# A selective-scan kernel on one core: the copy of each state's last column moves from ScalarE to GpSimd

## The reference, cut to what matters

```
def step(h, inp):
    u_t, d_t, b_t, c_t = inp
    dA = jnp.exp(d_t[..., None] * A)
    h = dA * h + (d_t * u_t)[..., None] * b_t[:, :, None, :]
    y = jnp.einsum('bkdn,bkn->bkd', h, c_t)
    return (h, y)
```

## Time and profile before

| | |
|---|---|
| time, median of 3 runs | 12323.96 us (12319.58 to 12334.21) |
| the profiled execution, its own time | 12312.74 us |
| its span from first to last instruction | 12310.8 us |
| DVE busy, share of the span | 88% |
| PE busy, share of the span | 86% |
| POOL busy, share of the span | 77% |
| ACT busy, share of the span | 72% |

### The profile page before, as it was taken

One profiled execution on the slowest core, in us unless ns is written; L12 is line 12 of the kernel. 1 busy time (PEld: TensorE's weight loads), 2 busy tenths in 40 slices (PEclk: granted clock), 3 DMA queues, 4 the chain that ended last, 5 costly groups with the idle time before them and its releaser, 6 DMA issues. The chain is left out here.

```text
span 12310.8 us, 117469 instructions
## 1 busy us (share of the span) xinstructions
PE 10629.6 (86%) x33046; PEld 4749.1 (39%) x33046; DVE 10864.5 (88%) x7695; ACT 8817.2 (72%) x18292; POOL 9515.3 (77%) x4213
## 2 busy tenths in 40 slices
PE   7888888888888888888888888888888888888888
PEld 2443334343344433434334443334433344334443
DVE  7999779997799978999789997899968999689996
ACT  5777667776677766777667776677766777667776
POOL 4999459994599945999459994599936999369993
PEclk9999989999899998999989999999998999999999
DMA  4677446764467644677446774477745677356773
GB/s 140 214 222 214 117 133 215 221 215 110 134 214 222 214 109 139 215 221 214 104 143 215 221 214 101 148 215 219 214 97 149 216 220 215 94 153 215 219 215 91
DMA packets 677497, 2203.72 MB, mean 179 GB/s; under 512 B 165008, under 2 KB 167056, under 8 KB 665424
## 3 DMA queue, kind: packets, MB, share of 16 engines
q1 hardware_dynamic: 676848, 2196.22, 61.3%
HBM read 2098.86 MB, written 67.11 MB: 176 GB/s over the span
## 5 line engine op out<-in xcount | busy, mean ns | idle before, releaser
L1309 POOL TENSOR_TENSOR state<-state,c_sb 128x1024 f32<-128x1024 f32 x3072 | 7180.7, 2363 | 610.5 <-ACT carry L1143 528.5
L1065 PE MATMUL ps<-state,wt 128*128 128x512 f32 x12288 | 5863.5, 614 | 350.5 <-ACT ya L1136 233.4
L1278 DVE TENSOR_TENSOR_SCAN state<-decay,carry,ps 128x1024 f32<-128x1024 f32 x1728 | 4006.7, 2340 | 41.1
L1065 PEld LDWEIGHTS ps<-state,wt 128*128 128x128 f32 x12288 | 2324.5, 196 | 2778.8 <-issue 2105.3
L1199 ACT ACTIVATE decay<-delta,a_neg 128x1024 f32<-128x1024 f32 x2304 | 2638.6, 1146 | 0.2 <-issue 0.2
L1186 ACT ACTIVATE dbu_t<-du_t,b_t 128x128 f32<-128x128 f32 (+1 forms) x8128 | 2301.4, 360 | 0.0
L1143 ACT COPY carry<-state 128x1 f32<-128x1 f32 x3072 | 572.0, 186 | 2136.4 <-DVE state L1278 2127.1
L1265 DVE TENSOR_TENSOR ps<-ps,du 128x1024 f32<-128x1024 f32 x1544 | 1866.2, 1209 | 97.9 <-PE ps L1015 97.6
L1298 POOL TENSOR_TENSOR dbu<-b_sb,du 128x1024 f32<-128x1024 f32 x768 | 1811.5, 2359 | 0.0
L1015 PE MATMUL ps<-parts,sel 114*128 114x512 bf16 (+1 forms) x3088 | 944.7, 388 | 679.6 <-DVE state L1278 673.1
L1278 DVE TENSOR_TENSOR_SCAN state<-ps,carry,dbu 128x1024 f32<-128x1024 f32 x576 | 1343.2, 2332 | 68.1 <-ACT ps L1199 47.6
(11 more groups left out here) (218 smaller groups left out, 9959.1 us busy)
## 6 DMA issues: line engine op xcount, KB each, us to landing
c_sb<-bc SPq DMA_DIRECT2D x2048, 512.0 KB, 4.6
c_sb<-bc SPq DMA_DIRECT2D x2048, 256.0 KB, 5.7
b_sb<-bc SPq DMA_DIRECT2D x512, 512.0 KB, 4.1
b_sb<-bc SPq DMA_DIRECT2D x512, 256.0 KB, 4.0
x_nat<-x SPq DMA_DIRECT2D x17, 1536.0 KB, 14.8
gates<-gate_a SPq DMA_DIRECT2D x8, 2048.0 KB, 6.8
x_tok<-x SPq DMA_DIRECT2D x288, 48.0 KB, 1.9
gn<-gn_t SPq DMA_DIRECT2D x8, 1536.0 KB, 7.1
```

The lines of the kernel that those rows point to most:

```text
L1065: mm = pe.matmul(py[:, q * CH:(q + 1) * CH], col("ident"), state[:, slot(g, n), q * CH:(q + 1) * CH], start=(n == 0), stop=False)
L1278: dve.tensor_tensor_scan(state[:, slot(g, n), way], rate, what, 0.0 if fresh else carry[:, n:n + 1], ALU.mult, ALU.add)\
L1309: pool.tensor_tensor(state[:, slot(g, n), :], state[:, slot(g, n), :], c_sb[:, n % CRING, :], ALU.mult).then_inc(S["weighted"], 1)
```

## The change

GpSimd makes the copy itself, directly ahead of the product of the same state, and raises `carried`. ScalarE no longer makes it. What is copied, and every other order, stays. GpSimd's product still waits for `carried`, which GpSimd itself now raises one instruction earlier; VectorE's scan of the next chunk waits for it as before.

```diff
                 @block.scalar
                 def _(act):
-                    for q in ("carried", "y_taken"):
-                        act.sem_inc(S[q], CREDIT)
+                    act.sem_inc(S["y_taken"], CREDIT)
...
-                    def carry_on(T, g, n):
-
-                        last = SC - 1 if T < 3 else 0
-                        act.wait_ge(S["scanned"], g * NS + n + 1 + CREDIT)
-                        act.copy(carry[:, n:n + 1], state[:, slot(g, n), last:last + 1]).then_inc(S["carried"], 1)
...
                                 if n + 2 - half in TURNS[1:]:
                                     times_b(T, g, n + 2 - half, half)
-                            if n > 0:
-                                carry_on(T, g, n - 1)
-                            elif previous:
-                                carry_on(previous[0], g - 1, NS - 1)
...
                     each_chunk(steps)
-                    carry_on(5, 6 * NSC - 1, NS - 1)
                     take_y(5, 0, 6 * NSC - 1)
...
                     pool.sem_inc(S["dbu_pooled"], CREDIT)
+                    pool.sem_inc(S["carried"], CREDIT)
+
+                    def carry_on(T, g, n):
+
+                        last = SC - 1 if T < 3 else 0
+                        pool.wait_ge(S["scanned"], g * NS + n + 1 + CREDIT)
+                        pool.tensor_copy(carry[:, n:n + 1], state[:, slot(g, n), last:last + 1])\
+                            .then_inc(S["carried"], 1)
...
                                 times_b(T, c, POOLED.index(n + 2))
+                            carry_on(T, g, n)
                             pool.wait_ge(S["carried"], g * NS + n + 1 + CREDIT)
```

## The result

The changed kernel takes 12703.19 us (median of 4 runs, 12697.84 to 12704.65) against 12324.76 us: a ratio of 1.0305, 95% interval 1.0288 to 1.0323. It is 378 us slower. The forecast was 295 us slower, 12620 us, with a range of 12480 to 12900.

The account below looks back on a forecast made before the run. VectorE set the pace by a little; GpSimd would become the bound. At 0.21 us more per state, scans take 1201.4 us against 1164.5, 295 us more for eight: 12608, plus 11 to the median, said as 12620 us, range 12480 to 12900.

Parts of the forecast that it names:

- GpSimd becomes the bound: In the eight scans, GpSimd's added work overfills its idle time, so it sets the pace: 1201.4 us per scan against 1164.5.
- The idle time swallows the first part: In each scan GpSimd has 48.5 us idle, some 40 us of it usable, to set against 80.6 us of added work.
- The price of a state, x = 0.12 + 0.09: GpSimd's added time per state: 0.12 us for the copy, 0.09 us for the product's wait; together 0.21, ends 0.18 and 0.32.
- The waits for C: GpSimd's waits for loads of C from memory, kept in full at 6.5 us per scan.
- Starts, not lengths: GpSimd's products counted by spacing of starts, 2.316 us each; by recorded lengths the total would be 12796 us.
- The long quarter adds nothing: VectorE's quarter with `du`, 13.79 us against GpSimd's 12.42, fits in 1.8 us of slack and is won back afterwards.
- ScalarE's relief: Dropping ScalarE's 3072 copies, 572.0 us, lets `decay` of state 3 start earlier: 11 us at most, counted as nothing.
- The dearer copy: Rival: GpSimd's copy costs like its 128x128 product, 0.49 us, x 0.59 us, total 13786 us; values from 0.32 up, chance 0.09.
- The rival that the copy hides: GpSimd's own wait is free, x is 0.103 us, about fitting its idle time; 12324 us, chance 0.08.
- The faster rival: ScalarE is never late with `decay` for states with `dbu`, VectorE's 63.6 us of waits vanish; 12260 us, chance 0.05.
- rival 4: The faster rival: VectorE's 63.6 us of waits for ScalarE's `decay` vanish; 12260 us, chance 0.05.
- rival 3: The rival that the copy hides: GpSimd and VectorE run level, time stays at 12324 us, chance 0.08.

Follow-up runs that it names:

- e_no_own_wait: Changed kernel, but GpSimd's copy reads a constant tile instead of the state, so the product need not wait for it; 12361.92 us, ratio 1.0027.
- e_on_vector: Kernel before, but VectorE makes each copy right behind its scan and waits for that scan; ScalarE and GpSimd make none; 12852.02 us, ratio 1.0421.

## Why the prediction was right, and where its size was off

**GpSimd becomes the bound: shown.** VectorE waits for it 543 times instead of 50, and it for VectorE only at each image's start. A second copy costs its full price, 0.24 us, with nothing hidden.

**The idle time swallows the first part: shown.** I had some 40 us per scan. The first and second copy differ by 45 us, and 4 moved copies of 16 cost nothing. The corner is not sharp, which I hadn't foreseen: probably some quarters are bound by one engine and some by the other with 8 and 12 copies, but I have not shown that.

**The price of a state, x = 0.12 + 0.09: mis-sized, and put together wrongly.** Measured is 0.247 us: 1212.3 us less 2.6 at the start and 3.1 for C, over 96 quarters, is 12.57 us instead of 11.58, and a fourth of the difference is 0.247. The rows give (12.56 - 11.58) / 4 = 0.245. In the prediction's own terms, a length and a gap, the length of the copy is what was too small: it is 0.185 us, like ScalarE's 0.186, where I had weighed it toward the memset of 0.103 and taken 0.12. The gap behind it is 0.08, about as I took it. From their sum, 0.265, some 0.02 come off, since the copy starts a little earlier than a product would.

The experiments divide the price by cause. Alone, the copy costs 0.14 us from its start to the next, less that 0.02: 0.12 us. That this is the number I took is luck, since I meant the copy's length. The own wait alone costs 0.127, not 0.09, since it takes away the 0.04 us of overlap besides adding the gap of 0.08. Either way x is 0.037 us too small, and 0.037 x 3072 = 114 us are missing from the forecast.

**The waits for C: too large.** I kept 6.5 us per scan, it was 24.6 / 8 = 3.1 us. The longer quarter gave the loads more time, which I had named and not counted; with two copies the waits shrink further, to 4.4 us in all. My 6.5 was the first image alone; the eight images before have 68.2 us, 8.5 per scan. It takes 27 us off. 295 + 114 - 27 = 382 us, the 382 us by which the scans grew.

**Starts, not lengths.** The sum by the starts, with the measured price, is the one that comes out. By the recorded lengths, 0.045 us too long 480 times a scan, it would be 170 us too high. The Trainium skill (Perfetto Trace Analysis, GPSIMD Engine Instruction) has this rule, and the trace agrees: in `e_no_own_wait` a copy recorded at 0.20 us is followed by the next start after 0.14.

**The long quarter adds nothing: shown.** The quarter with `du` took 13.36 us, and the waits behind it 0.27 and 1.00 us.

**ScalarE's relief: right sign, too small.** I said 11 us at most and counted nothing, since VectorE no longer sets the pace. Without any copy the kernel is 33 us faster, not all of it traced to ScalarE; in the changed kernel no such gain is seen.

**The rivals.** The dearer copy (0.32 us and more) is excluded by the measured 0.247. The rival that the copy hides needed a free own wait; it costs half of the price. Without it, in `e_no_own_wait`, the time did nearly come out as that rival had it, 12362 against 12324. The rule behind it in the Trainium skill (VectorE: DVE Perf Modes, The DRAIN you can't avoid) is that a semaphore after each of eight copies on VectorE cost nothing extra. It doesn't carry over to GpSimd here, nor to a copy behind a scan on VectorE: with the wait for its own scan VectorE goes from scan to copy in 2.38 us, and from scan to a multiplication without a wait in 2.25. Copies behind copies on VectorE, the page's own case, no run here has. The faster rival is excluded too: even with no copy anywhere the gain is 0.26%. A slip in the chances: half of rival 4's 0.05 beside rival 3's 0.08 makes 0.105 for "within 0.2%", not 0.09.

## What to carry to other kernels

Cut the busy shares to the stage before choosing an engine to take work: GpSimd's 77% was 96% where the work went. Before moving a small instruction, set its full cost, count times start-to-start price, against the idle time that the receiving engine has in that stage, and count an engine's wait for its own last instruction as a price of its own (0.127 us here on GpSimd, as much as the copy). On ScalarE the same dependency fell into a wait for the scan that existed anyway, and taking the copies out altogether gave 33 us. If the instruction must go to the full engine, put something else between it and the instruction that needs it: at 4 of 16 states that gave 70 us back.

## What the runs showed of the hardware

- A wait for the instruction just ahead on the same engine costs 0.127 us on GpSimd (four starts with three such waits take 9.65 us instead of 9.27) and about 0.13 us on VectorE (scan to copy 2.38 us, scan to a multiplication without a wait 2.25), though nothing is late.
- A copy of one column (128x1) on GpSimd occupies it 0.14 us from start to start, and is recorded 0.17 to 0.21 us long. On ScalarE it is recorded 0.186 us long, on VectorE 0.154 (`e_on_vector`).
